# Adjacency scatters of a four-layer graph network: adding counts to cleared cells, where they were written

## The chip, the cores and the metric

The kernel runs on one core of one Trainium2 chip, as one launch. The metric is the device time of a run in microseconds (us), without a profiler; lower is better. The median of three runs before the change is 4437.25 us (4429.48 to 4437.64).

## The reference, cut to what matters

A graph of 6,250 nodes and 100,000 edges goes through four graph layers. Edges are sorted by their destination `dst`, and destinations are drawn as 6250 u², so low node numbers have most of the edges.

```python
edge_index = jnp.stack([src, dst])
x = _layernorm(x + _L0_gnn_ref(x, src, dst, ...))                  # softmax over the edges of a node
x = _layernorm(x + _L1_gnn_ref(x, edge_index, edge_attr_4, ...))   # a message per edge, normed, summed by node
x = _layernorm(x + _L2_gnn_ref(x, edge_index, ...))                # two SAGE convolutions
x = _layernorm(x + _L3_gnn_ref(x, edge_index, ...))                # two more
```

Each of the four SAGE convolutions of the last two layers does the same with the edges:

```python
msg = x[src]
agg = jax.ops.segment_sum(msg, dst, num_segments=n_nodes)
agg = agg / jnp.maximum(cnt, 1.0)[:, None]
return agg @ Wl.T + b + x @ Wr.T
```

The edges are the same in all four, so the sum is a product with one matrix of counts: row src, column dst, value the number of edges from src to dst.

## The kernel before, in words

**Stages.** After a setup come two passes over the edges: SOFT (layer 0) and MESSAGE (layer 1). Each goes over 196 tiles of 512 edges (`ET` tiles of `TE` edges), a tile being four chunks of 128 edges, and each ends with a stage over the nodes in seven groups. Then come the four convolutions, which use the count matrix.

**The count matrix.** It lies in DRAM as `adj` (fp16): 51 jobs (49 tiles of 128 destination nodes and 2 joint jobs for runs that cross a tile of edges), each 128 partitions of source numbers by 51 blocks of 128 columns. During the SOFT pass SyncE clears it with 102 large DMAs from a tile of zeros (`clear`, L582). In the MESSAGE pass VectorE compares each edge's cell number with those of the edges around it (`count_copies`, L1650). That gives each edge the number of edges that share its cell; an edge that is not the first of its cell gets a mark, and its cell number is replaced by one of its own behind the matrix (`redirect`, L1661 to L1667, `elsewhere`). So no cell is the target of two edges.

**The scatters.** GpSimd (POOL) writes the counts with indirect DMAs of 128 elements of 2 bytes, one from each partition, to 128 cells of DRAM. There are 782 of them, one per chunk of 128 edges. `EARLY` = 392 are issued in the MESSAGE pass (`scatter_chunk`, L781), two per tile: `gather_and_scatter(t)` issues two gathers of source rows for tile t (L770), a scatter of chunk 0 of the earlier tile t-3, two more gathers, and the second scatter. They draw on `cell_ring` and `copies_ring`, rings of four tiles, and VectorE's `redirect` waits on `adj_made[s]` for the scatters of four tiles back. The other 390 are issued after the pass (L857), in batches of eight, from `cell_late` and `copies_late`.

**Who waits for them.** `batch_done(i - 1)` stands behind the issue of batch i: POOL waits until all of batch i-1 has landed (`late_made`) and then counts `adj_ready` up. SyncE's `fill_first` (L665 to L669) reads from `tile_ready` how many batches the matrix tile of 128 destinations needs, waits for `adj_ready` and loads the tile into one of four slots of SBUF. TensorE's `sum_up_first` (L1105 to L1113) waits for the slot and does the tile's job of convolution 1: 49 matmuls (L1111). The early scatters hold the first half of the edges, and by the square in the draw their destinations are below node 1,563, which is some 12 of the 49 tiles; the other tiles become ready one after another as late batches land.

The order on each engine is the program's; no scheduler or planner comes in. On POOL's queue, the late scatters stand behind the gathers of the rows' ends (L836) and nothing stands behind them.

Of the kernel before, what the change touches and what calls it, by code (L numbers as in the profile page):

```python
# [78 lines left out]
def build(nc, n_edges, x_in, chunk_last_in, node_rows_in, dst_cols_in, dst_before_in, dst_seq_in, src_cols_in, node_cols_in, next_row_in,  # L79
# [3 lines left out]
    ALU = mybir.AluOpType  # L83
# [32 lines left out]
    with ctx:  # L116
        def sb(name, shape, t=f32):
            return ctx.enter_context(nc.sbuf_tensor(name, shape, t))
# [4 lines left out]
        def sem(name):  # L123
            return ctx.enter_context(nc.semaphore(name))
# [145 lines left out]
        copies_ring = sb("copies_ring", [P, RING, NOW], f16)  # L270
# [3 lines left out]
        copies_late = late(P, LATE // 2).bitcast(f16)  # L274
# [121 lines left out]
        adj_made = [sem(f"adj_made{s}") for s in range(RING)]  # L396
        constants_kept = sem("constants_kept")
        late_redirected = sem("late_redirected")
        late_made, adj_ready = [sem(f"late_made{b}") for b in range(2)], sem("adj_ready")
# [140 lines left out]
        def _(sp):  # L540
# [44 lines left out]
            for p, kind in enumerate(PASSES):  # L585
# [4 lines left out]
                def load(u, h):  # L590
# [4 lines left out]
                    if kind == MESSAGE:  # L595
                        _, firsts = nc.values_load_multi_w_load_instructions(  # L596
                            first_rank[0:1, bass.ds(t * CH, 2 * CH)], engines=[mybir.EngineType.SP], min_val=0, max_val=NP,
                            skip_runtime_bounds_check_because="a count of runs, of which there are NP at most")
# [109 lines left out]
        def _(pool):  # L708
# [44 lines left out]
            for k in range(NT):  # L753
# [3 lines left out]
                                        in_offset=bass.IndirectOffsetOnAxis(ap=chunk_i[:, k:k + 1], axis=0))\  # L757
                    .then_inc(rows_landed[g // 2], 16)

            for p, kind in enumerate(PASSES):  # L760
# [18 lines left out]
                def scatter_chunk(t, c):  # L779
                    s = t % RING  # L780
                    pool.indirect_dma_start(  # L781
                        out=adj_all, out_offset=bass.IndirectOffsetOnAxis(ap=cell_ring[:, s, c:c + 1], axis=0),
                        in_=copies_ring[:, s, c:c + 1], in_offset=None).then_inc(adj_made[s], 16)

                def scatter(t):
                    pool.wait_ge(redirected, t + 1)
                    for c in range(NOW):
                        scatter_chunk(t, c)

                def gather_and_scatter(t):  # L790
                    wait(pool, e["turned"], t - RING + 1)
                    for c in range(NOW):
                        gather_chunks(t, range(c * CH // NOW, (c + 1) * CH // NOW))
                        if c == 0:
                            pool.wait_ge(redirected, t - 3 + 1)
                        scatter_chunk(t - 3, c)
# [5 lines left out]
                else:  # L802
# [9 lines left out]
                    for i in range(EXT):  # L812
                        pool.indirect_dma_start(
                            out=adj_all, out_offset=bass.IndirectOffsetOnAxis(ap=joint_cell[:, i:i + 1], axis=0),
                            in_=one_h[:, :], in_offset=None).then_inc(joint_ones_made, 16)
# [17 lines left out]
                for g in range(NG):  # L833
                    for k in range(g * GT, (g + 1) * GT):
                        wide = 2 * F if kind == SOFT else F
                        pool.indirect_dma_start(out=ends[:, k, 0:wide], out_offset=None,  # L836
                                                in_=soft_sums if kind == SOFT else sums,
                                                in_offset=bass.IndirectOffsetOnAxis(ap=end_row[:, k:k + 1], axis=0))\
# [4 lines left out]
                if kind == MESSAGE:  # L843
                    pool.wait_ge(late_redirected, 2)

                    def batch_done(i):
                        begun = sum(min(BATCH, SCATTERS - EARLY - k * BATCH) for k in range(i % 2, i + 1, 2))
                        pool.wait_ge(late_made[i % 2], 16 * begun)
                        pool.sem_inc(adj_ready, 1)

                    for s in range(RING):
                        pool.wait_ge(adj_made[s], 16 * NOW * EI)
                    pool.wait_ge(joint_ones_made, 16 * EXT)
                    pool.sem_inc(adj_ready, 1)
                    for i in range(BATCHES):
                        for c in range(i * BATCH, min((i + 1) * BATCH, SCATTERS - EARLY)):
                            pool.indirect_dma_start(  # L857
                                out=adj_all, out_offset=bass.IndirectOffsetOnAxis(ap=cell_late[:, c:c + 1], axis=0),
                                in_=copies_late[:, c:c + 1], in_offset=None).then_inc(late_made[i % 2], 16)
                        if i:  # L860
                            batch_done(i - 1)
                    batch_done(BATCHES - 1)
                if kind == SOFT:
# [4 lines left out]
                    for g in range(NG):  # L868
                        pool.wait_ge(n["dst_kept"], g + 1)
                        for k in range(GT):  # L870
                            at = dst_row[:, g * GT + k:g * GT + k + 1]
                            pool.indirect_dma_start(out=dst_table, out_offset=bass.IndirectOffsetOnAxis(ap=at, axis=0),
                                                    in_=dg[:, k, :], in_offset=None).then_inc(n["dst_stored"], 16)
# [1120 lines left out]
```

## Time and profile before

| What | Value |
|---|---|
| median of three runs, without the profiler | 4437.25 us |
| the profiled execution: span from first to last instruction | 5171.8 us |
| POOL busy in it | 2510.8 us (49%) |
| PE busy | 3159.9 us (61%) |
| DVE busy | 2679.3 us (52%) |
| indirect DMAs on POOL: 1568 gathers of source rows | 1492.1 us busy |
| 392 early scatters (L781) | 388.6 us busy, 991 ns each |
| 390 late scatters (L857) | 395.5 us busy, 1014 ns each |

For the profiled execution the span is the only time there is; it is 734.6 us longer than the median of the runs without the profiler. Busy time of an engine is the time of its instructions. A DMA that POOL issues counts as busy on POOL for as long as POOL works at issuing it, and the movement of its data comes after. "Idle before" a group of instructions is time in which the engine did nothing, with what ended it; "issue" there is a gap for which the profile shows no wait.

The stages by the trace: setup to 84 us, SOFT pass to 1,244, its node stage to 1,453, MESSAGE pass to 3,190, its node stage to 3,268, late scatters to 3,789, the rest of convolution 1 to some 4,160, convolutions 2 to 4 to the end.

### The profile page before, as it was taken

Reading aid. Unit: us, or ns where it says so; the run is one execution under the profiler, and the core shown is the slowest. Engines: PE = TensorE matmul, PEld = TensorE weight load, DVE = VectorE, ACT = ScalarE, POOL = GpSimd, SP = SyncE. Lnnn points to the kernel's source line nnn. Section 1 sums busy time; section 2 is a strip of 40 time slices with the busy share of each in tenths; the row PEclk is TensorE's granted clock in tenths of the full one; section 3 lists DMA queues with packets and bytes.
Section 4 is the critical chain, followed back from the end, with each engine's and each line's share of the span. In section 5 each row is a group of like instructions: output and inputs, shape, how many; then the busy total and the mean of one; then the engine's idle time right before and its main releaser. Section 6 shows DMA issues by size and latency. Waiting matters only on the chain.

```text
span 5171.8 us, 61853 instructions
## 1 busy us (share of the span) xinstructions
PE 3159.9 (61%) x18737; PEld 2317.1 (45%) x18737; DVE 2679.3 (52%) x5868; ACT 1560.3 (30%) x3684; POOL 2510.8 (49%) x2587
## 2 busy tenths in 40 slices
PE   1555555554755555555555554111159999999999
PEld 0333333333534344344344333100047777788777
DVE  4888888888645555555555556300001254433333
ACT  1777777776222222222222222100000011111000
POOL 7666666664666666666666666777720000000000
PEclk9999999999986667667667666555579999999999
DMA  5555555555134444444444443100037666666776
GB/s 183 192 198 191 195 194 194 192 192 164 56 98 111 112 121 111 116 117 111 114 118 112 111 118 85 58 0 0 13 126 282 215 218 245 247 248 251 259 276 228
DMA packets 387596, 797.88 MB, mean 154 GB/s; under 512 B 207412, under 2 KB 264600, under 8 KB 361128
## 3 DMA queue, kind: packets, MB, share of 16 engines
q1 hardware_dynamic: 239330, 586.35, 33.9%
q0 software_dynamic: 82320, 90.28, 7.9%
q10 hardware_dynamic: 65718, 118.62, 6.2%
q8 instruction: 93, 1.52, 0.1%
q14 instruction: 135, 1.11, 0.1%
HBM read 581.03 MB, written 213.92 MB: 154 GB/s over the span
## 4 chain that ended last, share of the span: by engine, by line
PE 25%; issue 23%; SPq 19%; DVE 3%; another core or an unknown queue 1%; DMA 0%; ACTq 0%; ACT 0%; DVEq 0%; POOL 0%
PE ps L1181 18%; SPq L626 14%; PE ps L1111 6%; SPq L601 1%; SPq L596 1%; SPq L622 1%; SPq L607 1%; SPq L617 1%; PE ps L1064 1%; ACTq L64 0%; DMA area<-adj 0%; PE ps L1083 0%; PE ps L1056 0%; DVE second L1650 0%
## 5 line engine op out<-in xcount | busy, mean ns | idle before, releaser
L770 POOL DMA_INDIRECT area<-src_table,early x784 | 752.5, 960 | 469.6 <-remote 225.5
L770 POOL DMA_INDIRECT area<-relu_table,early x784 | 739.6, 943 | 421.3 <-issue 212.4
L953 PE MATMUL ps<-ident,area 96*128 96x96 f32 x2352 | 441.4, 356 | 804.3 <-issue 555.4
L953 PEld LDWEIGHTS ps<-ident,area 96*128 96x128 f32 x2352 | 355.2, 213 | 939.2 <-issue 782.4
L1181 PE MATMUL ps<-second,area 128*128 128x288 bf16 x5194 | 652.1, 286 | 0.2 <-DVE second L1823 0.2
L1682 DVE TENSOR_TENSOR_SCAN area<-flags,area,ps 96x512 f32<-96x512 int8 x196 | 250.0, 1276 | 647.6 <-issue 552.0
L1181 PEld LDWEIGHTS ps<-second,area 128*128 128x128 f16 x5194 | 509.0, 98 | 128.5 <-DVE second L1823 0.5
L1650 DVE SCALAR_TENSOR_TENSOR second<-second,area,ps 128x512 bf16<-128x512 f32 x784 | 538.1, 741 | 0.0
L857 POOL DMA_INDIRECT adj<-out_ring x390 | 395.5, 1014 | 127.8 <-issue 127.8
L781 POOL DMA_INDIRECT adj<-copies_ring,cell_ring x392 | 388.6, 991 | 125.6 <-issue 118.9
L1111 PE MATMUL ps<-early,area 128*128 128x288 bf16 x2401 | 322.0, 292 | 204.9 <-issue 204.9
L1230 ACT ACTIVATE ps<-ps,msg_bias 96x512 f32<-96x512 f32 x196 | 126.7, 647 | 1042.5 <-remote 911.0
L942 PE MATMUL ps<-second,area 128*96 128x128 f32 x1568 | 378.1, 328 | 34.1 <-issue 33.8
L941 PE MATMUL ps<-ident,area 128*96 128x128 f32 x1568 | 382.4, 334 | 7.8 <-issue 7.1
L941 PEld LDWEIGHTS ps<-ident,area 128*96 128x96 f32 x1568 | 301.0, 215 | 170.3 <-issue 170.2
L925 PE MATMUL ps<-ident,area 128*96 128x128 f32 x784 | 208.0, 421 | 265.8 <-DVE second L1705 184.9
L1111 PEld LDWEIGHTS ps<-early,area 128*128 128x128 f16 x2401 | 236.7, 99 | 290.0 <-issue 231.7
L916 PE MATMUL ps<-attr,w_edge_parts 36*96 36x512 bf16 x392 | 235.3, 601 | 185.2 <-DMA attr<-attr_parts 118.7
L1695 DVE TENSOR_TENSOR_SCAN second<-ps,second 96x512 f32<-96x512 f32 x196 | 249.5, 1273 | 159.7 <-remote 153.7
L1181 PE MATMUL ps<-early,area 128*128 128x288 bf16 x2597 | 331.8, 286 | 0.0
L935 PE MATMUL ps<-second,w_ef_scaled 96*96 96x512 f32 x392 | 306.6, 875 | 0.4 <-issue 0.4
L942 PEld LDWEIGHTS ps<-second,area 128*96 128x96 f32 x1568 | 283.8, 210 | 23.5 <-issue 23.4
(330 smaller groups left out, 4709.0 us busy)
## 6 DMA issues: line engine op xcount, KB each, us to landing
area<-adj SPq DMA_DIRECT2D x147, 1632.0 KB
area<-adj SPq DMA_DIRECT2D x55, 1568.0 KB
adj<-early SPq DMA_DIRECT2D x102, 816.0 KB
soft_sums<-out_ring ACTq DMA_DIRECT2D x196, 384.0 KB
second<-key_dram SPq DMA_DIRECT2D x98, 512.0 KB
area<-dst_table SPq DMA_DIRECT2D x784, 48.0 KB
sums<-out_ring ACTq DMA_DIRECT2D x196, 192.0 KB
second<-caps_dram SPq DMA_DIRECT2D x98, 192.0 KB
```

Of the source, the lines that this page charges most:

```text
L626: sp.dma_start(dst_rows[:, s + c // CH, c % CH, :], dst_table[bass.ds(firsts[c], P), :])\
L770: pool.indirect_dma_start(out=src_rows[:, s, c, :], out_offset=None, in_=gather_table[p], in_offset=bass.IndirectOffsetOnAxis(ap=src_cols[ ...
L781: pool.indirect_dma_start(out=adj_all, out_offset=bass.IndirectOffsetOnAxis(ap=cell_ring[:, s, c:c + 1], axis=0), in_=copies_ring[:, s, c: ...
L857: pool.indirect_dma_start(out=adj_all, out_offset=bass.IndirectOffsetOnAxis(ap=cell_late[:, c:c + 1], axis=0), in_=copies_late[:, c:c + 1] ...
L935: nc.tensor.matmul(bank(s % 2, F), w_ef_scaled[:, :], h_ring[:, s % 2, :], start=True, stop=False)
L941: nc.tensor.matmul(ps[0:F, s % 2, at], src_rows[:, s, c, :], ident[:, :], start=False, stop=False)
L942: last = nc.tensor.matmul(ps[0:F, s % 2, at], dst_rows[:, s, c, :], rank_hot[:, s % 2, at], start=False, stop=c == CH - 1)
L953: last = nc.tensor.transpose(ps[:, b, c * F:(c + 1) * F], r[:, (s * CH + c) * P:(s * CH + c + 1) * P], ident[0:F, 0:F])
L1111: last = nc.tensor.matmul(bank(lane % 2, P, PARTS_F), slots[:, lane, s, :], y[:, s, :, :].rearrange("p c f -> p (c f)"), start=s == 0, sto ...
L1181: last = nc.tensor.matmul(bank(b, P, PARTS_F), slots[:, lane, s, :], y[:, s, :, :].rearrange("p c f -> p (c f)"), start=s == 0, stop=s == ...
L1650: last = v.scalar_tensor_tensor(same[:, c, :], keys[:, s, :], key[:, bass.ds(t * CH + c, 1)].bitcast(f32), around, ALU.is_equal, ALU.mult, ...
L1682: v.tensor_tensor_scan(out=slot(sum_ring, s), data0=flags[:, s, :], data1=bank(s % 2, F), initial=last_of(sum_ring, s), op0=ALU.mult, op1= ...
```

## The change

Both kinds of scatter get `compute_op=ALU.add`: the DMA adds the count to what the cell holds, where it wrote the count over it. The cells are cleared beforehand, as before, and each is the target of one edge, so the matrix is the same. The cells behind the matrix that take the marked edges' counts are not cleared, before or now, and nothing reads them. The two DMAs of `one_h` at the joints (L813) go on writing. No instruction comes, goes or moves on any engine.

```diff
@@ -780,7 +780,7 @@
                     s = t % RING
                     pool.indirect_dma_start(
                         out=adj_all, out_offset=bass.IndirectOffsetOnAxis(ap=cell_ring[:, s, c:c + 1], axis=0),
-                        in_=copies_ring[:, s, c:c + 1], in_offset=None).then_inc(adj_made[s], 16)
+                        in_=copies_ring[:, s, c:c + 1], in_offset=None, compute_op=ALU.add).then_inc(adj_made[s], 16)
@@ -856,7 +856,7 @@
                         for c in range(i * BATCH, min((i + 1) * BATCH, SCATTERS - EARLY)):
                             pool.indirect_dma_start(
                                 out=adj_all, out_offset=bass.IndirectOffsetOnAxis(ap=cell_late[:, c:c + 1], axis=0),
-                                in_=copies_late[:, c:c + 1], in_offset=None).then_inc(late_made[i % 2], 16)
+                                in_=copies_late[:, c:c + 1], in_offset=None, compute_op=ALU.add).then_inc(late_made[i % 2], 16)
```

## Rows read from the trace of the kernel before

**Rows 1.** Windows: the SOFT pass, the MESSAGE pass, the late scatters.
```profile
core 0: us, PE busy (x) PEld busy (x) DVE busy (x) ACT busy (x) POOL busy (x), PEclk, DMA share, GB/s
84.00:1244.00 1160.00, 605.66 (x2483) 390.80 (x2483) 949.38 (x1039) 851.53 (x1911) 738.82 (x784) 1.00 0.56 189
1453.00:3172.00 1719.00, 984.44 (x4438) 686.71 (x4438) 979.25 (x2734) 476.05 (x1160) 1133.52 (x1169) 0.70 0.44 114
3268.00:3789.00 521.00, 73.24 (x239) 44.09 (x239) 40.95 (x81) 15.00 (x29) 395.49 (x390) 0.52 0.06 16
```

**Rows 2.** POOL's groups of instructions, whole span: count | busy us, mean ns | idle before.
```profile
L770 POOL DMA_INDIRECT area<-src_table,early x784 | 752.5, 960 | 469.6 <-remote 225.5 <-issue 211.1 <-PE ps L942 33.1
L770 POOL DMA_INDIRECT area<-relu_table,early x784 | 739.6, 943 | 421.3 <-issue 212.4 <-remote 198.7 <-PE ps L925 10.1
L857 POOL DMA_INDIRECT adj<-out_ring x390 | 395.5, 1014 | 127.8 <-issue 127.8
L781 POOL DMA_INDIRECT adj<-copies_ring,cell_ring x392 | 388.6, 991 | 125.6 <-issue 118.9 <-DVE cell_ring L1666 6.6
...
L721 POOL MEMSET ones_bf<- 128x1 bf16 x1 | 0.1, 91 | 0.0
```

**Rows 3.** POOL's timeline in the MESSAGE pass: start us, us, instruction [idle before].
```profile
1488.17 0.96 POOL L770 DMA_INDIRECT area<-src_table,early  x1 [3.44 <-remote]
1489.44 0.95 POOL L770 DMA_INDIRECT area<-src_table,early  x1 [0.31 <-issue]
1490.70 0.99 POOL L781 DMA_INDIRECT adj<-copies_ring,cell_ring  x1 [0.30 <-issue]
```

**Rows 4.** Timeline of the late stage: PE's matmuls and POOL's last scatter.
```profile
3786.08 0.40 PE L1111 MATMUL ps<-early,area 128*128 128x288 bf16 x1 [2.40 <-issue]
...
3787.76 1.09 POOL L857 DMA_INDIRECT adj<-out_ring  x1 [0.30 <-issue]
3788.88 0.40 PE L1111 MATMUL ps<-early,area 128*128 128x288 bf16 x1 [2.40 <-issue]
```

**Rows 5.** Chain of waits that ended last, its longest pieces: start us, us, what.
```profile
3816.18 186.06 PE ps L1111 x1504
4002.25 6.00 PE ps L1120 x49
4008.25 90.05 PE ps L1111 x735
4098.32 14.10 DMA area<-adj
```

**Rows 6.** The same chain in the MESSAGE pass, us 2290 to 2330.
```profile
2291.57 0.71 SPq L626
2292.28 0.71 SPq L626
```

**Rows 7.** DMA queues from us 84 to 1244: packets, MB, share of 16 engines.
```profile
q0 software_dynamic: 25038, 38.53, 14.0%
```

**Rows 8.** DMA queues from us 3300 to 3550, and the issues there.
```profile
q0 software_dynamic: 6249, 0.06, 1.9%
...
adj<-out_ring POOLq DMA_INDIRECT x196
```

**Rows 9.** A small load's time from issue to landing, us.
```profile
early<-chunk_last_dram SPq DMA_DIRECT2D x1, 4.0 KB, 1.6
```

**Rows 10.** Windows: convolutions 2 to 4, columns as in the first group.
```profile
4104.00:5172.00 1068.00, 1047.14 (x8578) 841.25 (x8575) 430.83 (x1605) 119.69 (x420) 0.00 (x0) 1.00 0.68 244
```

## The prediction

> **What bounds the kernel now.** I read the table by stages first, then POOL's groups, then the chain of waits, and only then single DMAs. The change touches 782 DMAs of POOL and nothing else, so the question is in which stages POOL sets the pace, and what one of these DMAs will take.
>
> By the windows [rows 1] POOL is busy 738.8 of 1160 us in the SOFT pass, 1133.5 of 1719 in the MESSAGE pass and 395.5 of 521 behind the late scatters; PE and DVE are at 57% in the MESSAGE pass, PE at 14% in the late stage. In convolutions 2 to 4 POOL does nothing and PE is busy 1047 of 1068 us [rows 10]; the change can't reach that stretch. Behind each indirect DMA lies a gap of 0.30 us before the next [rows 3], so POOL's own pace is about 1.27 us per DMA: a tile of the MESSAGE pass, four gathers and two scatters, costs it 4 x 1.26 + 2 x 1.29 = 7.6 us, 1490 us for 196 tiles. POOL waits on others only for 225.5 + 33.1 + 6.6 = 265 us in the MESSAGE pass and 198.7 + 10.1 = 209 us in the SOFT pass [rows 2].
>
> The profiled execution is 5171.8 us long and the median of the runs is 4437.25, 734.6 less, so I have to say which of its waits a run without the profiler has. Two things look like the recorder's. While scatters run, SyncE's small steps follow each other every 0.71 us [rows 6], and PE issues one matmul in 2.80 us with no wait that the profile names [rows 4]. From us 3816.18 on, 27 us after the last scatter, the same matmuls take 186.06 / 1504 = 0.124 us each [rows 5]. If I take out what follows from these, it is: POOL's 209 and 265 us of waiting in the two passes; and in the late stage the 27 us, plus the 282 us of convolution 1 from 3816.18 to 4098.32 less the last three jobs of 49 matmuls (6 us each), since the other jobs could have run while later batches were scattered. That makes 209 + 265 + 291 = 765 us, 30 more than the difference. So I hold, as an inference, that in a run without the profiler **POOL is nearly always at work from the first gather to the last scatter**, and that convolution 1 ends a few jobs after the last scatter. Then every ns that a scatter takes longer on POOL is paid 782 times.
>
> **The change, part by part.**
>
> *Issue on POOL, 782 times.* Today a scatter handles 128 elements: one read of the count and one write of the cell each, 256 accesses to be described. An add must also read the cell: 384. The trace shows no adding DMA, so I bound it. From below: nothing, since a gather of 128 rows of 384 bytes takes 0.943 to 0.960 us and a scatter of 128 elements of 2 bytes 0.991 [rows 2]; what is moved hardly shows in the issue. Less than nothing I exclude, but for a small chance, because the add has all the accesses of the write. From above: a whole further indirect DMA with its gap, 0.98 + 0.30 = 1.28 us, or, without the gap and the start, 0.98 - 0.09 = 0.89 us, where 0.09 is POOL's shortest instruction [rows 2], as the price of starting one. I take the value by the count of accesses: the part that can grow is 0.89 us for 256, and half as many come on top, **+0.44 us**. That lies between the two nearest rows, a scatter for nothing and a scatter again. POOL waits for nothing in the late stage but the batch before the one just issued, some ten us old.
>
> *Early, 392 of them:* 392 x 0.44 = 172 us. In the profiled execution POOL's 265 us of waiting would swallow all of it; in a run without the profiler, by the paragraph above, next to nothing is left to swallow it and it is paid in full.
>
> *Late, 390 of them:* 390 x 0.44 = 172 us. Nothing lies beside this stage that could take its place: PE has its jobs only as batches land.
>
> *The DMA engines.* Today 196 scatters are 6249 packets in 1.9% of 16 x 250 us, 12 ns each [rows 8], about two packets per engine and scatter. The gathers' packets, with reads from DRAM, take 14.0% of 16 x 1160 us over 25038, 104 ns [rows 7]. An add reads DRAM, and if each cell became a packet of its own at 104 ns, an engine would need 8 x 104 = 0.83 us per scatter, under POOL's 1.27 and hidden. It would cost from 1.27 / 8 = 159 ns on; at 1.6 us a cell, the time of a small load from issue to landing [rows 9], one after another, it would be 12.8 us per scatter.
>
> *The waits behind.* `redirect` waits for scatters of four tiles back and POOL for a batch back, ten us; an add that lands one or two us later is covered by both. If it came later than that, POOL would stall once per batch. No DMA is moved on a queue, and SyncE's loads of matrix tiles shift with `adj_ready`.
>
> Sum: 172 + 172 = 344 us, **4437.25 + 344 = 4781 us**. Against the profiled execution's own 5171.8 us I expect about 172 more, the late part, 5344: the early part is lost there in waits that the recorder makes.
>
> The Trainium skill speaks against a sum by accesses. In GPSIMD Engine Reference, section When to use GPSIMD, it says that two cores share the issue of such a DMA, one describing the reads, the other the writes; in DMA: Bandwidth & Descriptors, section SDMA does more than copy, that an add is an elementwise reduction of two streams. By that the core with the reads has twice the work and the other the same: either +0.89 us (+696 us, 5133) if the reads are the longer half, or nothing if they are done early. Neither row here can tell the halves apart; both outcomes stand below as rivals.
>
> **The rivals.**
>
> *No change.* The reads of the cells are described beside the writes, which take as long as ever, and the engines hide the rest. For it: gather and scatter cost the same to 5% although one looks up its addresses on the reading side, the other on the writing side, and DMA engines are 6% busy in the late stage [rows 1]. Against: 128 further addresses must be made by somebody. It decides if the issue stays under 1.0 us. Time: 4437 us, within 9 us, since 11 ns per scatter are 0.2%. The Trainium skill, in DMA: Bandwidth & Descriptors, section Anatomy of one DMA, says that generating descriptors costs little and that many can be emitted before it shows, which would give this time; the like prices of gather and scatter agree, and no row here has more accesses per DMA.
>
> *The issue doubles.* +0.89 to +1.28 us, 782 times: +696 to +1001 us, 5133 to 5438. For it: an indirect read plus an indirect write is a gather plus a scatter. Against: the start and the addresses are shared.
>
> *The engines become the bound.* Each cell is read, added and written before the next. At 208 ns a cell, twice a gather's packet, a scatter takes 1.66 us: late +0.39 x 390 = 152 us, early hidden, as two such scatters and four gathers (2 x 1.66 + 4 x 2 x 0.104 = 4.2 us) fit into 7.6: 4589. At 400 ns it is 3.2 us: late +753, early just hidden (6.4 + 0.8 = 7.2): 5190. At 1.6 us a cell, +9000. For it: the smallest load takes 1.6 us, and 2-byte accesses are the worst case. Against: gathers read many rows at 104 ns a packet, so reads overlap.
>
> *Faster, or the add is not done as one.* A mechanism for faster I can't name; at most the add would go out like the write.
>
> **How the numbers follow.** Forecast (0.2 to 0.7 us per scatter, 4593 to 4985): 0.42. No change: 0.22. Doubled issue: 0.18. Engines: 0.14, half of it above 5440. Faster: 0.04. The range reaches from no change, 4428, to the end of the doubled issue, 5440, and leaves out some 0.11. The likeliest case alone would have 4593 to 4985. A measurement can tell 0.2%, some 9 us, from no change; slower by more than that are forecast, doubling and engines, 0.42 + 0.18 + 0.14 = 0.74, within it 0.22, faster 0.04.
>
> **What would show it.** In the profile of the changed kernel the two scatter groups should stand at 1.4 us mean in place of 0.99 and 1.01, with 0.30 us gaps, the gathers unchanged; the window of late scatters should be 172 us longer and POOL's waits in the MESSAGE pass shorter by about as much as its scatters grew. If the means stay and the late window grows, the engines are the bound: POOL's gaps, or packets of the software queue, would show it. If the means stay and nothing grows, it is no change. I am wrong in the early part if the time grows by 390 times the difference only: then the MESSAGE pass is not POOL's, even without the profiler.

## The result and the profile after

The changed kernel takes 4920.73 us (median of 4 runs, 4915.45 to 4922.79) against 4437.44 (4 runs): 483 us more, a ratio of 1.109 with a 95% interval of 1.107 to 1.110. The forecast was 4781 us, slower, with a range of 4428 to 5440; the direction was right, the cost per scatter too low.

One thing has to be said before the rows are compared. The first profile of the kernel before (5171.8 us) is far longer than any of its runs, and the profile of the changed kernel (4913.7 us) is as long as its own. So I took a second profile of the unchanged kernel. It is 4438.7 us long, as its runs are, and the comparison below is with that one. What slowed the first profile is not shown; I take it to be the recording, because the kernel is the same.

POOL's groups in the second profile of the kernel before (columns as in [rows 2]):

```profile
L770 POOL DMA_INDIRECT area<-src_table,early x784 | 752.6, 960 | 240.7 <-issue 240.7
L770 POOL DMA_INDIRECT area<-relu_table,early x784 | 739.8, 944 | 239.0 <-issue 228.0 <-PE ps L925 11.0
L781 POOL DMA_INDIRECT adj<-copies_ring,cell_ring x392 | 388.6, 991 | 119.4 <-issue 116.4 <-DVE cell_ring L1666 3.0
L857 POOL DMA_INDIRECT adj<-out_ring x390 | 382.3, 980 | 126.9 <-issue 125.9 <-DMA adj<-out_ring 0.9
```

The same groups with the change:

```profile
L770 POOL DMA_INDIRECT area<-src_table,early x784 | 756.6, 965 | 241.0 <-issue 241.0
L770 POOL DMA_INDIRECT area<-relu_table,early x784 | 745.8, 951 | 238.9 <-issue 235.9 <-PE ps L925 3.0
L781 POOL DMA_INDIRECT adj<-copies_ring,cell_ring x392 | 637.8, 1627 | 119.4 <-issue 103.6 <-DVE cell_ring L1666 15.8
L857 POOL DMA_INDIRECT adj<-out_ring x390 | 610.2, 1565 | 121.2 <-issue 120.9 <-DMA adj<-out_ring 0.3
```

The early scatters grew by 637.8 - 388.6 = 249.2 us and the late ones by 610.2 - 382.3 = 227.9, together 477; the spans differ by 4913.7 - 4438.7 = 475. The counts, the gaps (0.30 us per DMA) and, within 1%, the gathers are the same. So the whole loss is POOL's issue of these 782 DMAs, and in these stages POOL pauses in neither kernel: the idle column holds hardly anything but the gaps, where [rows 2] had 225.5 us behind others in the MESSAGE pass alone. The loss also lies where the scatters are: from its first gather to its last scatter the MESSAGE pass takes 1751 us in place of 1498 (+253), and from first to last late scatter it is 727 in place of 505.5 (+222).

The windows say the same. The kernel before, second profile, SOFT pass, MESSAGE pass and late stage (columns as in [rows 1]):

```profile
84.00:1068.00 984.00, 616.20 (x2524) 396.86 (x2525) 959.07 (x1056) 857.57 (x1945) 739.71 (x784) 1.00 0.69 225
1258.00:2750.00 1492.00, 1020.90 (x4486) 742.05 (x4486) 990.48 (x2767) 491.72 (x1172) 1135.35 (x1170) 0.73 0.51 133
2830.00:3340.00 510.00, 356.64 (x2490) 269.35 (x2491) 87.85 (x187) 14.19 (x30) 383.32 (x390) 0.83 0.45 152
```

With the change, the MESSAGE pass and the late stage:

```profile
1258.00:3010.00 1752.00, 1082.96 (x4510) 791.81 (x4510) 996.69 (x2769) 494.55 (x1179) 1392.94 (x1176) 0.69 0.50 113
3090.00:3820.00 730.00, 381.64 (x2506) 279.00 (x2507) 80.92 (x179) 13.89 (x29) 610.17 (x390) 0.74 0.50 108
```

Before, 1135 us of POOL's work and 1170 gaps of 0.30 us are 1486 of the 1492 us of the MESSAGE pass; with the change 1393 + 353 = 1746 of 1752. In the late stage PE now does its jobs beside the scatters in both kernels (some 2490 and 2506 matmuls, where the slowed profile had 239, [rows 1]) and goes on for only a few behind the last scatter. The end of that stage in the chain of waits, kernel before, second profile (start us, us, what):

```profile
3344.71 13.04 DMA adj<-out_ring
3357.81 7.69 DMA area<-adj
3365.55 7.54 PE ps L1111 x49
```

And with the change:

```profile
3818.22 13.81 DMA adj<-out_ring
3832.10 7.84 DMA area<-adj
3839.99 9.08 PE ps L1111 x49
```

The last landing, the last load and the last job follow each other as before, 13 to 14 us, 8 us and one job. From its start the last add lands 0.8 us later than the last write, and 0.6 of these are its longer issue (1.56 us in place of 0.97).

### The profile page after: what moved, and what is told of

Its sections match the earlier page's. It is cut to its first block, busy times and chain, and to the rows that moved or that the text cites. A ratio compares the mean times of both kernels' runs of the same rounds, so it can differ in the third digit from the quotient of the medians.

```text
span 4913.7 us, 61853 instructions
## 1 busy us (share of the span) xinstructions
PE 3263.6 (66%) x18737; PEld 2416.2 (49%) x18737; DVE 2677.3 (54%) x5868; ACT 1560.7 (32%) x3684; POOL 2985.2 (61%) x2587
## 4 chain that ended last, share of the span: by engine, by line
POOL 34%; PE 22%; issue 10%; DMA 4%; DVE 3%; ACT 1%; DVEq 0%; POOLq 0%
PE ps L1181 18%; POOL adj L857 12%; POOL area L770 12%; POOL adj L781 10%; DMA area<-src_table,early 2%; DMA adj<-copies_ring,cell_ring 1%; DVE second L1650 1%; PE ps L941 1%; POOL area L836 1%; PE ps L942 1%; PE ps L1064 1%; ACT ps L1230 0%; DVE second L1640 0%; DMA adj<-out_ring 0%; DMA area<-sums,end_row 0%
## 5 line engine op out<-in xcount | busy, mean ns | idle before, releaser
L941 PE MATMUL ps<-ident,area 128*96 128x128 f32 x1568 | 479.3, 405 | 659.2 <-DMA area<-src_table,early 658.9
L941 PEld LDWEIGHTS ps<-ident,area 128*96 128x96 f32 x1568 | 341.3, 256 | 858.6 <-DMA area<-src_table,early 857.7
L781 POOL DMA_INDIRECT adj<-copies_ring,cell_ring x392 | 637.8, 1627 | 119.4 <-issue 103.6
L857 POOL DMA_INDIRECT adj<-out_ring x390 | 610.2, 1565 | 121.2 <-issue 120.9
L1111 PE MATMUL ps<-early,area 128*128 128x288 bf16 x2401 | 363.8, 323 | 340.7 <-DMA area<-adj 340.7
L953 PE MATMUL ps<-ident,area 96*128 96x96 f32 x2352 | 429.6, 349 | 127.0 <-ACT out_ring L1246 122.7
L1682 DVE TENSOR_TENSOR_SCAN area<-flags,area,ps 96x512 f32<-96x512 int8 x196 | 250.1, 1276 | 475.3 <-ACT dump L1234 474.5
L1111 PEld LDWEIGHTS ps<-early,area 128*128 128x128 f16 x2401 | 261.2, 110 | 443.2 <-issue 315.2
L942 PE MATMUL ps<-second,area 128*96 128x128 f32 x1568 | 454.3, 389 | 0.0
L1848 DVE TENSOR_REDUCE whole<-ps 128x96 f32<-128x288 f32 x49 | 22.4, 458 | 655.8 <-PE ps L1111 655.8
L925 PE MATMUL ps<-ident,area 128*96 128x128 f32 x784 | 210.8, 424 | 248.9 <-DMA area<-relu_table,early 172.3
L942 PEld LDWEIGHTS ps<-second,area 128*96 128x96 f32 x1568 | 354.3, 259 | 0.0
L1181 PE MATMUL ps<-early,area 128*128 128x288 bf16 x2597 | 331.8, 286 | 0.0
L1181 PEld LDWEIGHTS ps<-early,area 128*128 128x128 f16 x2597 | 254.0, 98 | 63.1
L925 PEld LDWEIGHTS ps<-ident,area 128*96 128x96 f32 x784 | 126.2, 189 | 307.8 <-DMA area<-relu_table,early 251.8
```

Of the source, the lines that this page charges most:

```text
L781: pool.indirect_dma_start(out=adj_all, out_offset=bass.IndirectOffsetOnAxis(ap=cell_ring[:, s, c:c + 1], axis=0), in_=copies_ring[:, s, c: ...
L857: pool.indirect_dma_start(out=adj_all, out_offset=bass.IndirectOffsetOnAxis(ap=cell_late[:, c:c + 1], axis=0), in_=copies_late[:, c:c + 1] ...
L925: last = nc.tensor.transpose(ps[0:F, s % 2, c * P:(c + 1) * P], src_rows[:, s, c, :], ident[:, :])
L941: nc.tensor.matmul(ps[0:F, s % 2, at], src_rows[:, s, c, :], ident[:, :], start=False, stop=False)
L942: last = nc.tensor.matmul(ps[0:F, s % 2, at], dst_rows[:, s, c, :], rank_hot[:, s % 2, at], start=False, stop=c == CH - 1)
L953: last = nc.tensor.transpose(ps[:, b, c * F:(c + 1) * F], r[:, (s * CH + c) * P:(s * CH + c + 1) * P], ident[0:F, 0:F])
```

## The experiments

**The kernel before, once more.** No edit.

> The kernel before, unchanged, for a second profile. Theory 'POOL's issue' (every scatter's time on POOL is paid because POOL never pauses from the first gather to the last scatter): where the recorder does not slow it, the span is close to 4437 us, POOL's waits on other engines in the MESSAGE pass fall from 265 to under 30 us, late scatters take 0.97 us each, and the late stage is about 496 us. Rival 'other engines': POOL still waits over 100 us in the MESSAGE pass, as the first profile had it, or the span is again near 5170 us.

Measured: 4440.45 us, span 4438.7. The rows stand above: POOL's waits on other engines in the MESSAGE pass come to 3 us, and the late stage is 506 us long from its first to its last scatter. The theory of POOL's issue holds; the waits of the first profile [rows 2, 4, 6] belong to that profile and not to the kernel.

**Only the early scatters add, and only the late ones.** In each of these kernels one of the two hunks is made and the other left out (0:128 is all the partitions).

```diff
# early only (cut to the line with the add)
-                        in_=copies_ring[:, s, c:c + 1], in_offset=None).then_inc(adj_made[s], 16)
+                        in_=copies_ring[0:128, s, c:c + 1], in_offset=None, compute_op=ALU.add).then_inc(adj_made[s], 16)
# late only (cut likewise)
-                                in_=copies_late[:, c:c + 1], in_offset=None).then_inc(late_made[i % 2], 16)
+                                in_=copies_late[0:128, c:c + 1], in_offset=None, compute_op=ALU.add).then_inc(late_made[i % 2], 16)
```

> Only the 392 early scatters add, the late ones write. 'POOL's issue': 392 x (1.627 - 0.991) = +249 us, 4687 us. Rival 'early part is swallowed' by POOL's waits in the MESSAGE pass: near 4437 us. Rival 'landing' (VectorE's ring of four tiles waits for the adds and holds the pass up, and the late stage costs nothing): +400 us or more, above 4840.

> Only the 390 late scatters add, the early ones write. 'POOL's issue': 390 x (1.565 - 0.967) = +233 us, 4671 us; early-only and late-only together give the whole 483. 'Early part is swallowed': nearly the whole +483, 4920 us. 'Landing' in the ring: under +80 us.

Measured against 4445.6 us of the kernel before on the same chip: early only 4689.9 us, +244, ratio 1.055 (1.053 to 1.057); late only 4665.9 us, +220, ratio 1.050 (1.048 to 1.051). Both are as the theory has them, to 6%. The two sum to 465 of the 483. By the profiled executions (4685.3 and 4664.0 us against 4438.7) they are 246.6 and 225.3, together 472 of 475, so most of the 18 us lies in the medians that are compared: the kernel before was itself 8 us slower on this chip. In the profile of early only, POOL's groups are:

```profile
L781 POOL DMA_INDIRECT adj<-copies_ring,cell_ring x392 | 637.5, 1626 | 119.5 <-issue 106.7 <-DVE cell_ring L1666 12.8
L857 POOL DMA_INDIRECT adj<-out_ring x390 | 379.4, 973 | 125.5 <-issue 124.6 <-DMA adj<-out_ring 0.9
```

and of late only:

```profile
L857 POOL DMA_INDIRECT adj<-out_ring x390 | 608.8, 1561 | 121.3 <-issue 121.3
L781 POOL DMA_INDIRECT adj<-copies_ring,cell_ring x392 | 386.8, 987 | 119.6 <-issue 114.7 <-DVE cell_ring L1666 4.9
```

Each kind has its own price and doesn't touch the other. Both rivals, that the early part is swallowed and that VectorE's ring of four tiles holds the pass up, are refuted.

**Fewer rows.** What is the 0.6 us made of? The scatters were cut to 64, 32 and 16 partitions, adds of one kind beside writes of the other.

```diff
# 64 rows, early adds and late writes
-                        out=adj_all, out_offset=bass.IndirectOffsetOnAxis(ap=cell_ring[:, s, c:c + 1], axis=0),
-                        in_=copies_ring[:, s, c:c + 1], in_offset=None).then_inc(adj_made[s], 16)
+                        out=adj_all, out_offset=bass.IndirectOffsetOnAxis(ap=cell_ring[0:64, s, c:c + 1], axis=0),
+                        in_=copies_ring[0:64, s, c:c + 1], in_offset=None, compute_op=ALU.add).then_inc(adj_made[s], 16)
# ... and the late scatters, cut to their last line
+                                in_=copies_late[0:64, c:c + 1], in_offset=None).then_inc(late_made[i % 2], 16)
```

> Early scatters add, late ones write, each for the first 64 partitions only; the counts of the other 64 partitions are left out of the matrix. Theory 'reads beside writes' (reads and writes are described side by side, a fixed 0.37 us and 0.60 us for 128 of the longer side; an add has twice the reads): add of 64 0.97 us, as a write of 128; write of 64 0.67 us. 'By accesses' (start 0.09, then so much per access, one after another): write of 64 0.53 us, add of 64 0.85. 'Fixed price of an add': add of 64 stands 0.6 us above write of 64. 'Rows don't count': 0.97 and 1.6 as with 128.

> Early scatters write, late ones add, each for the first 32 partitions only; the counts of the other 96 partitions are left out of the matrix. 'Reads beside writes': write of 32 0.52 us, add of 32 0.67. 'By accesses': 0.31 and 0.47. 'Fixed price of an add': add of 32 stands 0.6 us above write of 32.

> Early scatters add, late ones write, each for the first 16 partitions only; the counts of the other 112 partitions are left out of the matrix. Theory 'start and rows' (from the runs with 128, 64 and 32 rows: an add is a start of 1.29 us and 2.6 ns a row, a write 0.84 us and 1.1 ns a row): add of 16 1.33 us, write of 16 0.86 us, so 0.44 us of the add's price has nothing to do with the rows. Rival 'steps' (the price goes by blocks of rows, 32 or more): as with 32 rows, write 0.88, or a fall well below the line, add under 1.2 us.

The scatters' instructions, with count: duration ns min/median/max, first and last start (what stands behind the semicolon can be left aside). With 64 rows, early adds and late writes:

```profile
L781 POOL DMA_INDIRECT adj<-copies_ring,cell_ring x392: 1397/1457/1476, 1276.4 to 2945.0; - x196
L857 POOL DMA_INDIRECT adj<-out_ring x390: 892/897/1479, 3025.7 to 3498.3; - x195
```

With 32 rows, early writes and late adds:

```profile
L781 POOL DMA_INDIRECT adj<-copies_ring,cell_ring x392: 860/882/887, 1282.8 to 2716.2; - x196
L857 POOL DMA_INDIRECT adj<-out_ring x390: 1306/1310/1898, 2799.2 to 3428.8; - x195
```

With 16 rows, early adds and late writes:

```profile
L781 POOL DMA_INDIRECT adj<-copies_ring,cell_ring x392: 1276/1345/1365, 1269.8 to 2892.9; - x196
L857 POOL DMA_INDIRECT adj<-out_ring x390: 831/836/1475, 2973.7 to 3422.4; - x195
```

And with all 128 rows, for comparison, first of the kernel before (second profile), then of the changed kernel:

```profile
L781 POOL DMA_INDIRECT adj<-copies_ring,cell_ring x392: 966/991/1005, 1276.0 to 2756.6; - x196
L857 POOL DMA_INDIRECT adj<-out_ring x390: 962/967/1592, 2839.2 to 3344.7; - x195
L781 POOL DMA_INDIRECT adj<-copies_ring,cell_ring x392: 1554/1629/1656, 1276.2 to 3010.0; - x196
L857 POOL DMA_INDIRECT adj<-out_ring x390: 1559/1563/2278, 3091.0 to 3818.2; - x195
```

A write's medians, late, go 967 (128 rows, second profile of before), 897 (64), 836 (16): 1.1 to 1.3 ns a row on a start of some 0.82 us. An add's, early, go 1629, 1457, 1345: 2.3 to 2.7 ns a row on a start of some 1.3 us. So of an early add's 0.64 us over a write, some 0.47 are there with hardly any rows and the rest is the rows' own price, about doubled. Why an add starts dearer on POOL, no run shows. None of the theories that the runs with 64 and 32 rows named was right as it stood: "reads beside writes" and "by accesses" make the start far too small (writes of 32 rows at 0.52 and 0.31 us against 0.88), "fixed price", the nearest, leaves out the slope (0.64 us above a write with 128 rows, 0.5 with 16), and "rows don't count" leaves it out altogether. The line drawn from three sizes foretold the fourth within 25 ns. The times of these kernels (one run each), 4584.87, 4512.61 and 4505.89 us (before: 4439.48, 4439.48 and 4444.95), are 145, 73 and 61 us more; the two groups' busy time on POOL changed by +156, +87 and +88, which is 10 to 27 us more. Two savings in the profiles stand against that: from the start of the last scatter to the end these kernels take 1082 to 1085 us where the kernel before takes 1094, and the gaps of the late stage come to 121 us in place of 127. With a quarter of the rows, the late adds alone still cost more than all the missing rows save.

Does POOL wait for the DMA engines in an add? The rows speak against it: the first early add of the changed kernel, at us 1276, takes 1.63 us like the rest, the fastest of the 392 takes 1.55, and with an eighth of the cells some 0.5 of the 0.64 us are still there.

**A gather that adds.** Is the add dear because a scatter's cells must be looked up a second time, to read them?

```diff
# cut to the end of the call
-                                                in_offset=bass.IndirectOffsetOnAxis(ap=end_row[:, k:k + 1], axis=0))\
+                                                in_offset=bass.IndirectOffsetOnAxis(ap=end_row[:, k:k + 1], axis=0),
+                                                compute_op=ALU.add if kind == MESSAGE else ALU.bypass)\
```

> The 49 gathers of the rows' ends after the MESSAGE pass (384 bytes a row, looked up on the reading side) add onto what lies in SBUF, so layer 1's sums are others than the reference's; all scatters write. 'Reads beside writes' (twice the reads, whichever side is looked up): about 0.95 + 0.60 = 1.55 us each. Rival 'second lookup' (the add is dear because a scatter's cells must be looked up on the reading side too): under 1.2 us, since SBUF rows need no lookup.

Measured: 4455.03 us against 4439.48. The gathers of the rows' ends, in the second profile of before (form as in the last fences):

```profile
L836 POOL DMA_INDIRECT area<-sums,end_row x49: 947/954/1594, 2762.6 to 2835.1; - x49
```

and as adds:

```profile
L836 POOL DMA_INDIRECT area<-sums,end_row x49: 1543/1570/2094, 2757.6 to 2852.8; - x49
```

The median grows by 0.616 us, the price of an adding scatter, although here only the source is looked up and the rows are 384 bytes long. (In the mean it is 0.476, from 1.210 to 1.686 us, since part of the plain gathers take up to 1.59 us anyway.) Neither the second lookup nor the bytes are what is paid for.

**Direct DMAs that add.** To see whether the price belongs to the index, 32 direct writes and then 32 direct adds of 128 rows of 2 bytes were put on POOL's queue behind the last batch.

```diff
# the semaphore direct_made is declared elsewhere
                     batch_done(BATCHES - 1)
+                    spare_cells = lambda i: adj_all[CELLS + (RING * NOW + i) * P:CELLS + (RING * NOW + i + 1) * P, :]
+                    for i in range(32):
+                        pool.dma_start(out=spare_cells(i), in_=one_h[:, :]).then_inc(direct_made, 16)
+                    pool.wait_ge(direct_made, 16 * 32)
+                    for i in range(32):
+                        pool.dma_start(out=spare_cells(i), in_=one_h[:, :], accum_op=ALU.add).then_inc(direct_made, 16)
+                    pool.wait_ge(direct_made, 16 * 64)
```

> The kernel before, and behind the last batch of late scatters, where POOL is otherwise done, 32 direct DMAs on POOL (no index, 128 rows of 2 bytes to cells behind the matrix) that write and then 32 that add. Theory 'price of any add': the direct add takes 0.5 to 0.65 us more than the direct write. Rival 'price of the index': direct add and direct write differ by under 0.25 us, the 128 rows' 1.5 ns each. The time of the run is that of the kernel before within 10 us, since only POOL does this, beside convolutions 1 to 4.

Measured: 4505.82 us against 4444.95, 61 us more where I had expected 10 at most. The time went to the matrix loads beside the small DMAs, for which TensorE waits: the largest took 73.3 us to land, where it takes 20.9 in the second profile of before. A second run spread each DMA's cells over the region behind the matrix:

```diff
+behind = adj_all[CELLS + RING * NOW * P:CELLS + (RING * NOW + LATE) * P, :].rearrange("(p i) a -> p i a", p=P)
+spare_cells = lambda i: behind[:, i, :]
# ... the two loops and waits as above, with a flag that allows spread cells
```

> As the run with direct DMAs behind the late stage, but each of the 32 direct writes and 32 direct adds goes to 128 cells that lie 784 bytes apart, as an indirect scatter's cells lie apart, where they were 256 bytes in one piece. Theory 'neighbouring cells' (that run's 61 us came from 2-byte accesses of 16 engines to the same bytes' surroundings): time within 10 us of the kernel before, landings under 8 us, and POOL's times are the price of the issue alone. Rival 'direct DMAs of 2 bytes clog the engines wherever they go': again 50 us or more and landings of 30 us. 'Price of any add': the direct add takes 0.4 to 0.65 us more on POOL than the direct write; 'price of the index': under 0.25 us more.

Measured: 4454.47 us against 4435.19, so 19 us more, between the two expectations but nearer to the first. The 32 spread writes in the trace, with their landing times:

```profile
L867 POOL DMA_DIRECT2D adj<-one_h x32: 537/540/594, 3363.5 to 3380.1; - x32
...
DMA to landing us min/median/max: 6.9/7.7/10.7
```

And the 32 spread adds:

```profile
L870 POOL DMA_DIRECT2D adj<-one_h x32: 921/6328/7490, 3391.0 to 3412.9; - x32
...
DMA to landing us min/median/max: 7.2/8.7/9.6
```

The adds' records overlap, so their median is not a price; the shortest, 0.921 us, is 0.38 above a write's 0.540, and all 32 take 29.35 us on POOL, 0.92 each. In the first of the two runs the shortest is the same and the 32 take 28.63 us, 0.89 each. That is just under the 0.4 that I had set as the bound for "any add" and well over the 0.25 for "the index". So a direct add pays some 0.36 to 0.38 us of an indexed add's extra 0.6, and the price doesn't belong to the index alone. That the rest comes with the index is not shown; the direct and the indexed DMAs differ in more than that.

No run pointed to a version that beats the kernel before: the start of each DMA, more than its rows, is what POOL pays for, and the number of chunks of 128 edges is the number of DMAs.

## Why the prediction was right, and where it was off

*POOL sets the pace from the first gather to the last scatter.* Right. It was inferred from the 734.6 us between profile and median [rows 1, 4, 5, 6], and the second profile shows it directly: 1486 of 1492 us of the MESSAGE pass are POOL's DMAs and their gaps.

*What the first profile had too much.* Nearly right. I had taken 209, 265 and 291 us out of the SOFT pass, the MESSAGE pass and convolution 1, 765 against a gap of 734.6. In the second profile the SOFT pass runs to 1,062 in place of 1,244, 182 less, and from its first gather to its last scatter the MESSAGE pass is some 235 us shorter. That leaves some 316 of the 733 for the node stages and convolution 1, against my 291. That the recording did it stays an inference.

*Nothing swallows the early part.* Right: early only +244 us.

*The issue grows by 0.44 us per scatter.* This is the step that failed in its size. "The part that can grow is 0.89 us for 256, and half as many come on top" took POOL's shortest instruction [rows 2], 0.09 us, as the price of starting a DMA. The start is some 0.82 us, and only 0.14 to 0.15 us go with 128 rows; an add has a start of its own, some 0.47 us dearer, and about twice the price a row. Measured: 0.636 early, 0.58 to 0.60 late, 0.61 us on average over 782, where the sum had 0.44. So the count of accesses was the wrong mechanism: the measured price lies between the two ends, and in the likeliest range of 0.2 to 0.7 us, because the bounds were wide, and that is luck. By the value that it needed, the sum is 782 x 0.61 = 477 us, 4914. The doubled issue (+0.89) did not come either.

*The DMA engines hide the rest.* Right, and one packet per cell fits the counts. The software queue in 100 us of the late stage, kernel before (second profile), with 78 scatters:

```profile
q0 software_dynamic: 2510, 0.03, 1.8%
```

and with the change, with 54:

```profile
q0 software_dynamic: 7799, 0.02, 20.5%
```

That is 32 packets per scatter before and 144 with the change, as many as 128 cells and one more for each of 16 engines would be. 20.5% of 16 x 100 us over 7799 are 42 ns a packet, where I had taken 104 from the gathers [rows 7]; nine packets an engine are 0.38 us of the 1.87 us from one scatter to the next.

*The waits behind.* Right that they cost nothing. Who waited for the early scatters (us, times), before (second profile) and with the change:

```profile
  DVE is_repeat L1661: 130.5, 92
  DVE is_repeat L1661: 265.5, 130
```

VectorE waits longer for its ring, but POOL's idle time before the early scatters is 119.4 us in both. Here the waiting engine is early, not late.

*The Trainium skill's two cores,* in GPSIMD Engine Reference, section When to use GPSIMD: neither of the two times that the prediction worked out by it came, neither nothing nor +0.89; no run here shows the two cores themselves. That generating descriptors costs little, as the Trainium skill has it in DMA: Bandwidth & Descriptors, section Anatomy of one DMA, agrees with the 1.1 to 1.3 ns a row of a write. But no change does not follow, since an add pays mainly at its start.

*Against the profiled execution* I expected 5344 us, early part lost; the profile came out at 4913.7, since it wasn't slowed as the first one was. The comparison with the first profile's span would have shown a slower kernel as faster by 258 us.

## What to carry to other kernels

When an engine that issues DMAs never pauses and everything behind it waits for the last of them, as here, every ns of each issue is paid, and the transfer's own price may not matter: find out the price of one issue and multiply. In this kernel an indirect DMA that adds costs 0.6 us more to issue than one that writes, and still 0.5 with 16 rows in place of 128, so write where the cell is known to be clear. And compare a profile's span with the run's time before using its waits: here the first profile was 735 us longer than the runs, and no run had its waits.

## What was not expected

The same program gave profiles of 5171.8 and 4438.7 us. In the slowed one, matmuls without any named wait came every 2.80 us.

The price of an indirect write depends little on its rows: a write of 16 rows takes 0.836 us on POOL, one of 128 rows 0.967.

32 direct DMAs of 128 times 2 bytes to 256 bytes in one piece landed after 30 us in the median (adds 41.7), and after 7.7 us (adds 8.7) with the cells 784 bytes apart; the run with the first kind was 61 us slower than the kernel before, the other 19. The two runs, one of each, differ in where the cells lie, so many small writes next to each other got in each other's way. What happens there in the memory, no run here shows.
